# Moving two steps of products in the periodic order of a chunked recurrence kernel

## The reference

```
h = table[x] + bias
h = h + attention(layernorm(h))
h = h + ffn(layernorm(h))

# attention, per batch b and head h (4 heads of 64), one step a token:
sa = S @ a_                              # a_ = -kk
S  = S * w_ + sa x b_ + v_ x k_          # b_ = kk * a
y  = S @ r_
# then: norm of y by head, * ln_w + ln_b, + rt * v, * gate, @ Wo
```

## Time and profile before

| | before |
|---|---|
| median of 3 runs | 482.14 us (479.24 to 486.59) |
| the profiled execution's own time | 479.76 us |
| span of that execution | 477.6 us |
| mean granted TensorE clock | 0.932 |
| TensorE matmul busy | 419.4 us |
| VectorE, ScalarE, GpSimd busy | 307.3, 200.2, 168.6 us |

### The profile page before, as it was taken

How to read it: one execution, slowest core, us unless ns; L and a number is a source line. 1 busy time by engine, 2 the same in 40 slices (tenths; PEclk the granted TensorE clock), 3 DMA queues, 4 the chain that set the end, 5 groups by cost and what they waited for, 6 DMA issues and landing times.

```text
span 477.6 us, 23442 instructions
## 1 busy us (share of the span) xinstructions
PE 419.4 (88%) x10651; PEld 337.1 (71%) x10651; DVE 307.3 (64%) x784; ACT 200.2 (42%) x418; POOL 168.6 (35%) x153
## 2 busy tenths in 40 slices
PE   0467999999999998999999999897896898999991
PEld 0345777777867876877777776786785797889981
DVE  3646878578478678859768857736387654545541
ACT  1276484484385376367347526411111341222220
POOL 4754422342433425215315313403002336545231
PEclk9996899999999999999999999876586899999996
DMA  8960000000000000000000000000004557656310
GB/s 275 323 268 1 3 5 4 4 4 5 27 4 5 27 3 5 25 5 4 4 27 4 5 26 5 3 26 5 4 16 137 219 190 254 208 188 195 111 44 23
DMA packets 14014, 32.15 MB, mean 67 GB/s; under 512 B 4121, under 2 KB 7068, under 8 KB 13788
## 3 DMA queue, kind: packets, MB, share of 16 engines
q1 hardware_dynamic: 10908, 22.47, 14.1%
q0 software_dynamic: 3008, 8.19, 5.2%
HBM read 25.50 MB, written 5.15 MB: 64 GB/s over the span
## 4 chain that ended last, share of the span: by engine, by line
PE 63%; issue 11%; DVE 7%; POOL 6%; ACT 6%; DMA 5%; POOLq 0%; DVEq 0%; ACTq 0%; SPq 0%
PE ps L970 7%; PE ps L977 6%; POOL out L371 4%; PE ps L982 4%; PE ps L1107 3%; PE ps L1391 3%; DMA arena<-kept,arena 2%; PE ps L989 2%; POOL arena L379 2%; PE ps L1249 2%; PE ps L1175 2%; PE ps L1058 2%; PE ps L1404 2%; PE ps L1081 2%; PE ps L1066 1%
## 5 line engine op out<-in xcount | busy, mean ns | idle before, releaser
L595 DVE SCALAR_TENSOR_TENSOR arena<-arena 128x256 f32<-128x256 f32 x96 | 47.8, 546 | 5.1 <-PE ps L1028 2.9
L1404 PE MATMUL ps<-arena 128*128 x184 | 44.4, 383 | 2.3 <-issue 1.3
L1391 PE MATMUL ps<-arena 128*128 128x128 f32 x368 | 46.3, 281 | 0.0
L1391 PEld LDWEIGHTS ps<-arena 128*128 128x128 f32 x368 | 45.6, 198 | 0.8
L371 POOL DMA_INDIRECT out<-arena x23 | 22.7, 985 | 51.2 <-DVE arena L929 50.6
L551 ACT ACTIVATE arena<-arena 128x512 f32<-128x512 f32 x23 | 14.5, 629 | 61.6 <-DVE arena L917 61.6
L1404 PEld LDWEIGHTS ps<-arena 128*128 128x128 f32 x184 | 33.1, 190 | 7.8 <-issue 4.0
L379 POOL DMA_INDIRECT arena<-kept,arena x23 | 22.5, 979 | 43.0 <-DMA kept<-arena 35.5
L970 PE MATMUL ps<-arena 128*128 128x256 f32 x128 | 35.5, 427 | 0.7 <-DVE arena L595 0.7
L977 PE MATMUL ps<-arena 128*128 128x256 f32 x128 | 34.7, 417 | 0.0
L322 POOL TENSOR_TENSOR arena<-arena 128x512 f32<-128x512 f32 x8 | 8.4, 1046 | 64.7 <-ACT arena L436 64.7
(11 more groups left out here) (315 smaller groups left out, 1046.3 us busy)
## 6 DMA issues: line engine op xcount, KB each, us to landing
arena<-W SPq DMA_DIRECT2D x23, 514.0 KB, 5.0
arena<-W SPq DMA_DIRECT2D x8, 512.0 KB, 8.3
kept<-arena SPq DMA_DIRECT2D x8, 256.0 KB, 2.4
arena<-W SPq DMA_DIRECT2D x4, 256.0 KB, 4.8
arena<-b SPq DMA_DIRECT2D x1, 1024.0 KB, 15.9
arena<-consts SPq DMA_DIRECT2D x1, 849.0 KB, 4.8
arena<-kept,arena POOLq DMA_INDIRECT x23, 4.8
out<-arena POOLq DMA_INDIRECT x23, 2.5
```

The costliest lines, as they stand in the source:

```text
L595: last = V.scalar_tensor_tensor(out=mix[j % 3][:, p, :], in0=xx[:, p].rearrange("p b t -> p (b t)"), scalar=mixed_by[MIXES[j]][:, p:p + 1] ...
L1391: last = mul(ps[:, 2 + b, m * 128:(m + 1) * 128], W1_s[i % WB][:, p * HID + m * 128:p * HID + (m + 1) * 128], x_sT[b][:, p, :], start=p == ...
L1404: last = mul(ps[:, 1, b * C:(b + 1) * C], hT[b][:, m, :], W2_sb[:, bass.ds(e * (HC * C) + m * C, C)], start=m == 0, stop=m == HC - 1)
```

## The change

Two steps of the list move. `Q.W0` comes ahead of `P.wup`, directly behind the steps of the third inverse round (`E.fold` has work for slab 0 only, `P.key` has none on TensorE). `Q.W1` comes ahead of `P.q`, `O.out` and `P.g`, directly behind `P.M` (between them `F.stats`, `F.rstd` and `E.out` have no work on TensorE, but for slab 0). No instruction is added or removed, and `LAST` stays.

```diff
-Q.X2:0 P.vga:1 F.xx:2 Q.T2:0 E.fold:2 P.key:1 P.wup:1 Q.W0:0 O.zT:-1 P.lg:1 N.rs:-2 Q.X3:0 P.cum:1 P.vc:1 N.lm:-2 P.decay:1
-P.rt:1 Q.T3:0 R.e:1 Z.l:-1 Q.A0:0 P.kP:1 P.ar:1 P.tokk:1 P.bP:1 Q.S0:0 P.k:2 P.M:1 F.stats:3 F.rstd:3 E.out:1 P.q:1 O.out:-1
-Q.W1:0 P.g:1 Z.c:-2 O.add:-1 Q.A1:0 P.tokb:1 P.masks:1 Q.S1:0 O.sq:0 P.r:2""".split()
+Q.X2:0 P.vga:1 F.xx:2 Q.T2:0 E.fold:2 P.key:1 Q.W0:0 P.wup:1 O.zT:-1 P.lg:1 N.rs:-2 Q.X3:0 P.cum:1 P.vc:1 N.lm:-2 P.decay:1
+P.rt:1 Q.T3:0 R.e:1 Z.l:-1 Q.A0:0 P.kP:1 P.ar:1 P.tokk:1 P.bP:1 Q.S0:0 P.k:2 P.M:1 F.stats:3 F.rstd:3 E.out:1 Q.W1:0 P.q:1 O.out:-1
+P.g:1 Z.c:-2 O.add:-1 Q.A1:0 P.tokb:1 P.masks:1 Q.S1:0 O.sq:0 P.r:2""".split()
```

## The result

The change makes the kernel slower: 498.15 us median of four runs (495.3 to 502.87) against 483.19 us for the kernel before on the same chip (four runs, 479.24 to 486.59); the ratio is 1.032, with a 95% interval of 1.026 to 1.038. The forecast was 478.2 us. The profiled execution took 495.5 us, 15.7 more than that of before.

What follows compares the result with a forecast made beforehand. TensorE's work, group behind group, was taken to bound turns 0 to 6. Savings of 1.6 us (Q.W0's move) and 1.1 us (Q.W1's), -2.7 against a median of 480.95, gave 478.2 us; range 473.5 to 484.5.

Steps and rivals of the forecast that it cites:

- the first part: What bounds the kernel: TensorE, busy 88% of the span, its groups following without a gap in turns 0 to 6.
- The entries of shapes: On TensorE, changing tile shape between neighbouring groups costs 0.12 to 0.18 us; the reordering removes some, 2.7 us in all.
- The step from P.M into 32-row tiles: On TensorE, Q.W1 directly behind P.M pays a change of small shapes, taken as 0.13 us between 0 and 0.18.
- ScalarE's queue: With the `w_s` copy ahead of P.wup's sigmoid, ScalarE is still free 0.1 us ahead of lg; R.e's wait stays 0.3 us.
- P.rt's wait for `rk`: VectorE's room ahead of P.rt is 0.06 to 1.8 us, under 0.3 in turns 4 and 5; 0.3 us taken off.
- Rival (a): At P.rt, VectorE takes back all the saving of Q.W0's move and half of Q.W1's; 480.4 us, chance 0.20.
- O.out's delay and the masks: O.out ends 2.15 us later, VectorE's masks move with it, and 1.3 us of room remains before Q.T0 would notice.
- VectorE's idle time before O.add: As a sign of being right, VectorE idles about 3.5 us before O.add in place of 1.41.
- rival (c): VectorE's masks, moved by 2.15 us, run slower beside GpSimd's products; no loss, or at worst 485.7 us; chance 0.08.
- Line 715: VectorE's idle time before the state of chunk 1 shrinks from 2.94 us to 0.6.
- Rival (d): The granted clock dips in turns besides turn 6, each costing 2.5 us; four of them make 488 us; chance 0.07.
- Rival (b): On TensorE, the shape costs of 0.13 to 0.18 us don't go away, or return at M to Q.W1; 481.0 us, chance 0.13.

## Why the prediction was wrong

The step that failed is in the first part: "the rest are single gaps of under 1.1 us. So in turns 0 to 6 the time is the sum of what TensorE does, one group behind the other". The same chain had gaps in the stretch that the earlier trace rows are from, ahead of the rows shown and between them:

```profile
141.63 0.65 issue
...
145.58 0.43 issue
```

I took the gaps with the releaser "issue" for accidents and left them out of the sum. They were 5.6 us, 4.3 of them in the turns, the sign of a limit that the kernel nearly touched, and I priced a group by its work and its neighbour's shape only, never by how many instructions it asks for in how short a time. The order of before had large products between Q.T2 and Q.W0 and between P.M and Q.W1; putting the large ones together brought the small ones together. In the profiled execution the gaps grew from 5.6 to 17.9 us, by 12.3, where 2.7 us were saved.

Point by point:

- The entries of shapes (0.12 to 0.18 us) and their savings were right in turn 2, each to 0.02 us. The line 1323 went from 0.59 to 0.44, P.g from 1.06 to 0.86. The step from P.M into 32-row tiles, taken as 0.13, didn't show as more: line 1249 took 1.04 as before.
- ScalarE's queue held: the chain to R.e still starts at the end of lg, and R.e's wait is the same, some 0.3 us.
- P.rt's wait for `rk` did not grow; TensorE lost so much ahead of it that VectorE had more room, not less (0.8 to 3.8 us over the seven turns, 0.06 to 1.8 before). Rival (a) was thus not tested.
- O.out's delay and the masks went as worked out but for two sizes. VectorE's idle time before O.add is 4.7 us in turn 2 in place of the 3.5 forecast, most of it because a block gap of 0.93 us stands in Q.W1. Line 673 takes 0.90 us, 0.49 more than its 0.41 beside nothing, and the same in every turn from 1 to 6; so the contention of rival (c) exists and fits in the room given to it. The prediction had priced it from a cast of 0.75 and 0.17 us and said that these times agree with the rule; that cast has one input, so they agree only if it ran in a 2-port mode, which no row shows. Line 715 lost its whole idle time where 0.6 us was forecast to remain.
- Rival (d) came in part: the clock fell in turns 1 and 4 too, which was named as a sign of failure. It cost 3.3 us in the two, and not 2.5 in each of four. Rival (b) is refuted by the entries themselves.
- None of the rivals had the mechanism that came. Those with the right sign were (c), which cost nothing, and (d), which gave 3.3 of the loss. The range, 473.5 to 484.5, held no term for a limit outside the engines' work. The chance of 0.03 for slower by over 2% was far too low, for the same reason.

## What to carry to other kernels

Ask of each stretch not only how long it takes but how many instructions it holds. Small float32 products (4 instructions each) run through 256 instructions in some 2 us, while over a longer stretch a block took 3.5 us or more to come; a large product between them is cover for that, and moving it away is not free. Gaps whose releaser is "issue" deserve to be located before they are left out: count the instructions from one to the next, and if it is a multiple of 256, the supply is a bound. The times of the packets on the instruction queue then show whether each gap ends a fixed time behind one. An edit that only shifts the queue (empty instructions ahead of the first wait) tells it from any dependency.

## What was not expected of the hardware

- Once TensorE had caught up with the supply, a block of 256 instructions came 3.47 to 4.02 us after the one before it, with one transfer of 16.4 KB each, and TensorE began it 1.20 to 1.62 us after the transfer had ended. The transfers began at least 3.24 us apart. The order of the kernel before lived within this by an average of 3.9 us a block.
- An empty instruction cost TensorE's queue 60 ns (32 in 1.93 us) behind small products, and next to nothing (0.13 us for 32) behind 1.93 us of large ones.
- The granted clock fell for 3.4 us at a time inside the turns of the changed kernel. It is not the gaps alone that bring this: the run with 256 empty instructions ahead had 17 gaps and no such fall between 50 and 309 us.
- Not tried: fewer instructions for the same work, which the gaps suggest as the real remedy.
